# Output projection of an attention block by feature tiles over four units, with the residual as an identity in a folded matrix

## What is computed

```python
x = x + attention(cond(x, ...))          # attention ends in: out @ w_o.T + b_o
x = x + ffn(cond2(x, ...), W_base, b_base, ...)
# cond2: base = x @ W.T, plus gated low-rank terms
# ffn:   x_flat @ W_base.T + b_base, plus gated low-rank terms
```

## Time and profile before

| | us |
|---|---|
| median of 3 runs | 1196.9 |
| lowest, highest | 1192.68, 1198.27 |
| profiled execution | 1195.03 |
| its span, first to last instruction | 1193.2 |
| PE busy | 1159.9 (97%) |
| DVE, ACT, POOL busy | 720.0, 422.0, 208.4 |
| DMA | 107.79 MB, mean 90 GB/s |

### The profile page before, as it was taken

The page is one execution under the profiler, slowest core; times in us unless marked ns, Lnnn a source line. Parts: engine busy times, 40 slices in busy tenths (PEclk is TensorE's granted clock), DMA queues, the critical chain, the costliest instruction groups (busy, mean ns, idle before and its releaser), DMA issues.

```text
span 1193.2 us, 18765 instructions
## 1 busy us (share of the span) xinstructions
PE 1159.9 (97%) x6920; PEld 1040.4 (87%) x6920; DVE 720.0 (60%) x1222; ACT 422.0 (35%) x1196; POOL 208.4 (17%) x133
## 2 busy tenths in 40 slices
PE   8999999999999999999989999999999899999998
PEld 8999988888888888888879998888887688888886
DVE  5312128878788888888874227444445866666664
ACT  5212124455545555555454223212123422222221
POOL 0000114433343344444350002000000000000000
PEclk9999999999999999999999999999999899999999
DMA  6111032111111111110323114555544322222212
GB/s 251 37 37 53 9 100 80 45 45 61 44 45 51 44 44 44 44 53 26 102 80 107 55 71 169 184 173 180 178 175 159 124 107 106 106 102 85 80 71 89
DMA packets 42151, 107.79 MB, mean 90 GB/s; under 512 B 5106, under 2 KB 16242, under 8 KB 42098
## 3 DMA queue, kind: packets, MB, share of 16 engines
q1 hardware_dynamic: 42098, 107.07, 25.6%
HBM read 73.50 MB, written 33.55 MB: 90 GB/s over the span
## 4 chain that ended last, share of the span: by engine, by line
PE 91%; DVE 5%; ACT 1%; DMA 1%; issue 1%; POOL 1%; SPq 0%; DVEq 0%; ACTq 0%; POOLq 0%
PE psum L1024 22%; PE psum L1643 13%; PE psum L389 13%; PE psum L1976 13%; PE psum L1396 8%; PE psum L2037 4%; PE psum L1086 4%; PE psum L1956 4%; PE psum L1056 3%; PE psum L1071 2%; PE psum L1043 1%; PE psum L1103 1%; PE psum L1659 1%; DVE low L894 1%; DVE rows L1563 1%
## 5 line engine op out<-in xcount | busy, mean ns | idle before, releaser
L1024 PE MATMUL psum<-p_h,c_high_low 128*128 128x512 f32 (+1 forms) x768 | 196.4, 359 | 0.5 <-DVE qkv L980 0.5
L1024 PEld LDWEIGHTS psum<-p_h,c_high_low 128*128 128x128 f32 x768 | 133.5, 188 | 13.3 <-issue 0.7
L389 PE MATMUL psum<-c_high_low,w_h 128*128 128x256 f32 x768 | 135.3, 286 | 5.0 <-ACT w_h L499 4.9
L389 PEld LDWEIGHTS psum<-c_high_low,w_h 128*128 128x128 f32 x768 | 117.2, 195 | 5.2 <-issue 5.2
L1396 PE MATMUL psum<-chunk,rows 128*128 128x384 f32 (+1 forms) x576 | 107.3, 342 | 4.8 <-DVE rows L1266 2.4
L1396 PEld LDWEIGHTS psum<-chunk,rows 128*128 128x128 f32 x576 | 102.6, 190 | 5.5 <-issue 5.4
L1024 PE MATMUL psum<-p_l,c_high_low 128*128 128x512 f32 (+1 forms) x384 | 104.3, 366 | 0.0
L389 PE MATMUL psum<-c_high_low,w_l 128*128 128x256 f32 x384 | 100.3, 286 | 0.0
L1643 PE MATMUL psum<-rows,ring 128*128 128x512 f32 x384 | 93.0, 397 | 0.0
L1643 PE MATMUL psum<-rows,at 128*128 128x512 f32 x384 | 90.4, 391 | 0.0
L1643 PEld LDWEIGHTS psum<-rows,ring 128*128 128x128 f32 x384 | 71.3, 188 | 17.2 <-DVE ring L1588 0.5
(11 more groups left out here) (182 smaller groups left out, 2308.5 us busy)
## 6 DMA issues: line engine op xcount, KB each, us to landing
ring_plain<-in_x_t SPq DMA_DIRECT2D x32, 256.0 KB, 2.6
attn_scratch<-ring_plain SPq DMA_DIRECT2D x16, 512.0 KB, 2.7
scratch_plain<-attn_scratch SPq DMA_DIRECT2D x16, 512.0 KB, 5.4
x_tok<-in_x_tok SPq DMA_DIRECT2D x16, 512.0 KB, 4.3
x_scratch<-x_out SPq DMA_DIRECT2D x16, 512.0 KB, 5.9
x_t_scratch<-x_t SPq DMA_DIRECT2D x16, 512.0 KB, 2.7
raw<-x_t_scratch SPq DMA_DIRECT2D x16, 512.0 KB, 4.1
rest<-x_scratch SPq DMA_DIRECT2D x16, 512.0 KB, 4.1
```

The costliest lines, as they stand in the source:

```text
L389: mm = pe.matmul(to, stationary, moving, start=start and n == 0, stop=k == KT - 1 and n == len(passes) - 1, skip_group_check=True)
L1024: mm = pe.matmul(to, sx[:, k, :], moving(w, n, k), start=first, stop=False, skip_group_check=True)
```

## The change

The projection's operands change roles. A slice is now 128 features of the attention output for four units (128 x 512, 512 KB before as rows of 4 KB, now 256 KB in pieces of 512 bytes), and it is the moving operand; stationary is a 128x128 block of w_o. Contraction is the outermost loop inside a group of four units: for each of eight slices all eight feature tiles are multiplied, each into its own bank. The result has features on partitions, as the feed-forward wants it. Transposes, `x_scratch`, `turned`, `add_bias` and `add_base_bias` are gone. `residual` is one instruction per tile: bank + bias (one number per partition) + x, with x loaded transposed. The residual of the feed-forward is no longer added from DRAM: `FoldFFN.products` adds an identity to the folded matrix, one 128x128 matmul of `eye` with itself on the diagonal of each of eight results, and `rest` loads b_base, broadcast to all partitions. Three buffers hold split slices (SPLIT) and four the raw ones (RAW). Five weights are split ahead of the fold's last results (EARLY), three behind them. The feed-forward's first splits are spread over the last slices, the last `residual` stands behind them.

```diff
         if k == KT - 1:
+            at = self.diagonal(s, i)
+            if at is not None:
+                mm = pe.matmul(self.tile(n, width)[:, at:at + P], self.eye, self.eye, start=False, stop=True, skip_group_check=True)
             mm.then_inc(self.done, 1)
         return mm
+    def diagonal(self, s, i):
+        at = i * P - FOLD_COLS[s][1]
+        width = FOLD_COLS[s][0] - (GATED if s == 0 else 0)
+        return at + (GATED if s == 0 else 0) if 0 <= at < width and i < KT else None
...
+    ORDER = (0, 1, 5, 6, 3, 4, 2, 7)
+    BANK_OF = (0, 1, 2, 3, 7, 4, 5, 6)
+    EARLY = 5
+    GROUP = 4
+    GROUPS = UNITS // GROUP
+    SLICES = KT * GROUPS
+    SPLIT = 3
+    RAW = 4
...
-    def low_attn(self, dve, u):
-        high, low = self.at[u % 2]
-        dve.wait_ge(self.at_high, u + 1)
-        dve.tensor_tensor(low, by_tile(self.at_raw), high.bitcast(F32), ALU.subtract).then_inc(self.at_low, 1)
+            engine.wait_ge(self.at_done, (KT - 1) * (n // KT) + n % KT + 1)
+    def load_attn(self, sp, n):
+        if n >= self.RAW:
+            sp.wait_ge(self.at_low, n - self.RAW + 1)
+        source = self.a["attn"][self.units(n // KT), :, self.features(self.ORDER[n % KT])].rearrange("u p t -> p u t")
+        sp.dma_start(self.by_unit(self.raw[n % self.RAW]), source).then_inc(self.at_in[n % self.RAW], 16)
...
+        act.wait_ge(self.at_in[n % self.RAW], 16 * (n // self.RAW + 1))
+        if n >= self.SPLIT:
+            self.slice_done(act, n - self.SPLIT)
+        elif n == self.SPLIT - 1:
+            act.wait_ge(self.fold.chunk_free, self.fold.free(self.fold.STEPS - 1, 4))
+        else:
+            act.wait_ge(self.fold.chunk_low, KT * self.fold.STEPS)
+        act.activation(self.at[n % self.SPLIT][0], self.raw[n % self.RAW], ACT.Copy).then_inc(self.at_high, 1)
...
+    def load_x(self, sp, g):
+        if g > 0:
+            sp.wait_ge(self.x1_stored, 16 * KT * g)
+        for i in range(KT):
+            sp.dma_start(self.by_unit(self.x[i]), self.a["x_t"][self.units(g), :, i, :].rearrange("u p t -> p u t")).then_inc(self.x_in, 16)
...
+    def multiply(self, pe, g, m):
+        n, k = KT * g + m, self.ORDER[m]
+        pe.wait_ge(self.at_low, n + 1)
+        if g == 0:
+            pe.wait_ge(self.w_low, k + 1)
+        (ah, al), (wh, wl) = self.at[n % self.SPLIT], self.weight(k)
+        for i in range(KT):
+            if m == 0 and g == 0:
+                pe.wait_ge(self.fold.out, self.fold.TILES * self.fold.STEPS - 6 + i - (i >= HALF))
+            elif m == 0:
+                pe.wait_ge(self.x1_ready, KT * (g - 1) + i + 1)
+            cols = self.features(i)
+            for p, (w, s) in enumerate(((wh, ah), (wh, al), (wl, ah))):
+                mm = pe.matmul(self.psum[:, self.BANK_OF[i], :], w[:, cols], s, start=m == 0 and p == 0, stop=m == KT - 1 and p == 2, skip_group_check=True)
+            if m == KT - 1:
+                mm.then_inc(self.tile_done, 1)
+        if m < KT - 1:
...
+        dve.wait_ge(self.x_in, 16 * KT * (g + 1))
+        for i in range(KT):
+            dve.wait_ge(self.tile_done, KT * g + i + 1)
+            dve.scalar_tensor_tensor(self.x[i], self.psum[:, self.BANK_OF[i], :], self.bo[:, i:i + 1], self.x[i], ALU.add, ALU.add).then_inc(self.x1_ready, 1)
...
+    TURN = 9
+    BEFORE_END = wo.SLICES - wo.SPLIT - 2
...
+        sp.wait_ge(fold.chunk_low, KT * fold.STEPS)
+        for n in range(wo.RAW):
+            wo.load_attn(sp, n)
+        for k in range(KT):
+            wo.load_weight(sp, k)
+        sp.dma_start(wo.bo, wo.a["b_o"].rearrange("(k p) -> p k", p=P), allow_slow_non_contiguous=True).then_inc(wo.bo_in, 16)
+        wo.load_x(sp, 0)
+        for n in range(wo.RAW, wo.SLICES):
+            wo.load_attn(sp, n)
+            if n > KT and n % KT == wo.RAW:
+                wo.store(sp, n // KT - 1)
+            elif n > KT and n % KT == wo.RAW + 2:
+                wo.load_x(sp, n // KT)
+                if n < 2 * KT:
+                    ff.load_raw(sp, 0)
+        wo.store(sp, wo.GROUPS - 1)
...
+        for k in range(wo.EARLY, KT):
+            wo.high_weight(act, k)
+        for n in range(wo.SPLIT - 1, wo.SLICES):
+            wo.high_attn(act, n)
+            if n >= BEFORE_END:
+                ff.begin_high(act, n - BEFORE_END)
+        ff.begin_high(act, wo.SPLIT + 2)
...
+        for k in range(wo.EARLY, KT):
+            wo.low_weight(dve, k)
+        for n in range(wo.SPLIT - 1, wo.SLICES):
+            wo.low_attn(dve, n)
+            if n >= TURN and n % KT == TURN % KT:
+                wo.residual(dve, n // KT - 1)
+            if n >= BEFORE_END:
+                ff.begin_low(dve, n - BEFORE_END)
+        ff.begin_low(dve, wo.SPLIT + 2)
...
-            sp.wait_ge(self.wo.x1_biased, UNITS)
-            sp.wait_ge(self.wo.x1_turned, 2 * UNITS)
-            sp.wait_ge(self.wo.x1_stored, 16 * BPU)
+            sp.wait_ge(self.wo.x1_stored, 16 * KT * self.wo.GROUPS)
         else:
             sp.wait_ge(self.out_stored[u], 16 * p)
-        sp.dma_start(self.rest[:, u, :], self.a["x1"][BPU * p + u, :, :]).then_inc(self.rest_in[u], 16)
+        sp.dma_start(self.rest[:, u, :], self.a["b_base"].partition_broadcast(P)).then_inc(self.rest_in[u], 16)
...
+    def begin_high(self, act, n):
+        for name in (("t1",), ("t2",), ("a11", "a12"), ("a21", "a22"), ("s1", "s2"), ("s3", "s4", "t3", "t4"))[n]:
+            if name in self.TERMS:
+                self.high_term(act, self.TERMS.index(name))
+            else:
+                self.high(act, 0, name)
+    def begin_low(self, dve, n):
+        for name in ((), ("t1",), ("t2",), ("a11", "a12"), ("a21", "a22"), ())[n]:
+            if name in self.TERMS:
+                self.low_term(dve, self.TERMS.index(name))
+            else:
+                self.low(dve, 0, name)
+        for name in ((), (), (), ("s1",), ("s2",), ("s3", "s4"))[n]:
+            self.sums(dve, 0, name)
+        if n == 5:
+            for name in self.SUMS:
+                self.low(dve, 0, name)
+            self.wo.residual(dve, self.wo.GROUPS - 1)
+            self.low_term(dve, 2)
...
-        if p == 0 and name in ("p5", "p6"):
-            pe.wait_ge(self.wo.x1_t_out, 2 * UNITS)
+        if p == 0 and name == "p1":
+            pe.wait_ge(self.wo.x1_ready, self.wo.SLICES)
...
+        pe.wait_ge(wo.x1_ready, wo.SLICES - KT + BPU)
         pe.wait_ge(fold.gate2_low, 1)
         pe.wait_ge(fold.out, fold.TILES * fold.STEPS)
-        ff.gates(pe, 0, 0)
-        wo.turn(pe, UNITS - 1)
-        ff.gates(pe, 0, 1)
+        for u in range(BPU):
+            ff.gates(pe, 0, u)
```

More of the change, by code:

```diff
@@ L1171, in second_rooms @@
         z = st.enter_context(nc.sbuf_tensor("z", [P, BPU, EXP, ER], F32))
[L1172 removed]
+        eye = st.enter_context(nc.sbuf_tensor("eye", [P, P], F32R))
+    return Second(scratch, chunk, rows, gates, b11, t1, g, b22, b21, t2, t3, t4, small, z, eye)
 def middle_rooms(nc, twins):
@@ L1590, in begin_high, with store @@
+    def store(self, sp, g):
+        for i in range(KT):
+            sp.wait_ge(self.x1_ready, KT * g + i + 1)
+            sp.dma_start(self.a["x1_t"][self.units(g), :, self.features(i)].rearrange("u p t -> p u t"), self.by_unit(self.x[i])).then_inc(self.x1_stored, 16)
     def begin_high(self, act):
-        for n, k in enumerate(self.ORDER):
+        for k in range(self.EARLY):
             self.high_weight(act, k)
-            if n == 0:
-                self.high_attn(act, 0)
+            if k < self.SPLIT - 1:
+                self.high_attn(act, k)
```

278 lines of the change are left out of this document (74 added, 204 removed).

## The result

| | before | after |
|---|---|---|
| median, 4 runs each | 1197.59 us | 1177.49 us |
| lowest, highest | 1192.68, 1199.24 | 1175.81, 1177.80 |
| ratio | | 0.9836, 95% interval 0.9805 to 0.9867 |
| profiled execution, span | 1195.03, 1193.2 | 1175.81, 1174.0 |

The forecast was 1176 us, in 1170 to 1187; the sum of its steps, made against the profiled execution, was -20.6 us, and the two profiled executions differ by -19.2.

A forecast was written before the change was run, and what follows sets the result against it. PE was taken as the bound in the projection, with the seams before and behind it. Terms -13.6 + 0 + 0.9 + 2.0 - 9.9 = -20.6 us against 1196.9 gave 1176 us, range 1170 to 1187.

The forecast's parts named there:

- transposes and handovers: Projection: fifteen sets of eight transposes leave PE, 13.1 us, with about 0.5 us of handovers between units; -13.6 us.
- matmul pace: Projection: 768 matmuls before and after, start-to-start kept at 230.6 ns; 0 us, ends -2.8 and +2.2.
- identities: Folds: eight added 128-column matmuls on PE, two of them in the attention stage; +0.9 us (0.5 to 1.1).
- seam in front: Projection's start: first slice's tiles 5, 6 and 7 wait for the last three fold results; +2.0 us.
- late slices: Inside the projection: slice 15 lands at 19 us after a group's end, before PE wants it; 0 us.
- seam behind: Projection's end to the up-gates: shrinks from 29.1 to 19.2 us, -9.9 us; ends -11.3 and -2.6.
- the rest: From the first up-gate to the end: no term in the sum, so 0 us.
- 11.4 us: Projection: further shrinkage estimated from the skill's 215.7 ns at 512 columns, left out of the sum.
- near 732 to 736: Projection's start: sign expected, three short PE waits on the fold's results at these times in us.
- 288 GB/s: Projection's transfers in 512-byte pieces: full-use rate taken from the fold's loads, eight transfers in 7.3 us.
- at full clock: Seam behind the projection: sign expected, up-gates some 19 us after the last slice without the lower clock.
- Nothing on PE: Biases and scratch: rest loads the base bias instead of x1, same size and count; no PE time.

The follow-up runs named there:

- two of eight: Kernel before with two instead of eight transposes per projection unit; median 1187.19 us over 4 runs.
- raw first: Changed kernel with the next pair's raw loads at the head of the feed-forward's DMA queue; median 1174.59 us over 4 runs.
- the identity's side alone: Kernel before with only the eight identity matmuls and base bias in rest, base-bias sums and x1 stores gone; median 1195.27 us, ratio 0.9986.

## Why the prediction was right

| step | predicted | measured |
|---|---|---|
| transposes and handovers | -13.6 | -13.5 (120 x 0.111 = 13.3 from two of eight; with the pace it makes up the stage's -12.5) |
| matmul pace | 0, ends -2.8 and +2.2 | -1.0 |
| identities | +0.9 | +0.6 in the fold, by their price 0.2 ahead of it |
| seam in front | +2.0 | +2.0 |
| late slices | 0 | 0, margin 18 us |
| seam behind | -9.9 | -9.3 |
| the rest | 0 | +1.6 |

*Pace.* A slice of 24 takes 5.50 us from start to start (748.02 to 759.02 is two slices), 229.1 ns, against 230.6 predicted. By slice it is 228.8 ns with the moving values in `at`, 228.9 and 229.6 in `ring`; before, with the stationary values there, it was 227.5 and 233.4 inside a unit, 230.4 in the mean, and 768 times the 1.3 ns between them is the table's 1.0 us. So the difference by buffer is nearly gone; whether it was the buffers that made it no run here shows, for the pairs of banks alternated with them. The 215.7 ns of the Trainium skill's section Back-to-back issue gap (TensorE: Matmul & The Clock Gate), which the section gives for an isolated matmul, is reached by no slice; its 11.4 us would have been wrong by 10.

*Seam in front.* The three short waits came where they were forecast, 733.4, 734.8 and 736.2 against "near 732 to 736"; the third start is 2.0 us late, of which 1.2 are listed as waits.

*Transfers.* Slice 15 landed 19.4 us behind the group's end, 19 forecast. The form that I bounded by 288 GB/s ran at 298 at a share of 0.98. The Trainium skill's section Latency and other measured facts (DMA: Bandwidth & Descriptors) keeps 207 GB/s for a row pitch of 512 KiB from partition to partition. Here partitions are 4 KB apart, and only the four pieces of one partition are 512 KiB apart, so the prediction took the figure to a case that it was not measured for; there was no such loss.

*Seam behind.* This term was mis-sized, in two places. The up-gates came 20.0 us behind the stage, not 19.2: the last stores landed 6.4 us behind it instead of 5.2, and raw at 15.2 instead of 14.1. The up matrix, which I had left out of that queue, was issued at 909.69 while they were under way, but that it delayed them is not shown: with raw first it comes later, raw stands in its place, and they land at 6.4 all the same; without the identities it stands where it did, and they land at 5.7. And the text said "at full clock": it saw that the wait would stay but gave it no price in clock, which was +1.6 us in the rest. The pace, 1.0 us better than the forecast, made up for part of these 2.2 us; in that the closeness of the forecast is luck. The account of the seam before was off by a little, too: of the stretch of 6.8 us at the lower level (938.7 to 945.5), 1.3 lay in the wait for z, so it cost about 2.7 us and not 3.5. With that the 9.1 us from 29.1 to 20.0 come out: 5.4 less idle time (0.98 + 2.97 + 4.07 to 2.59), 0.9 of transposes, 2.7 of clock. The kernel before, by stretch (columns as in the earlier trace rows):

```profile
938.80:940.00 1.20, 0.00 (x0) 0.00 (x0) 1.03 (x6) 0.92 (x2) 0.00 (x0) 0.50 0.00 0
940.00:945.40 5.40, 5.39 (x14) 4.33 (x15) 4.90 (x8) 1.10 (x3) 0.00 (x0) 0.50 0.00 0
945.60:948.30 2.70, 2.70 (x13) 2.23 (x12) 0.69 (x1) 1.12 (x2) 0.00 (x0) 1.00 0.00 0
```

*What the parts are worth.* The stage's 12.5 us come with the form of the projection. Of the seam's 9.3, the identity's side alone gave 3.3 in one trace of the kernel before, at 0.8 on PE, and 2.5 of them hang on where the lower clock fell; in ten runs it was worth 0.1 to 3.1 us in all. The form of the projection without the identity was not run, so the seam's gain is not divided further. The prediction's "Nothing on PE" for biases and scratch left out the 0.8 us by which z comes earlier without the bias sum.

## What to carry to other kernels

Price each wait that a change leaves, not only those that it removes: here 2.6 us of waiting cost 4.2, and a DMA issued three places earlier gave 3.5 of it back. Where the granted clock reacts to waits, a microsecond removed on another engine can be worth three or none, so read gains by stage, from stage to stage of the traces, and look at the granted clock of each stage before trusting a median. And try a suspected limit of transfers by adding traffic until it bites: that gives the margin in microseconds.

## What I had not expected of the hardware

The lower clock does not follow every equal wait. Behind the wait of 2.97 us ahead of the last transposes the kernel before stayed at the full level, and three variants of it, with 2.96 to 2.98, did not. Ahead of the up-gates, waits of 2.4 to 2.7 us were followed by it five times in five; three waits of 1.8 to 1.9 (two there, one ahead of z) were not. The stretch at the lower level cost 1.6 to 3.1 us there and 2.7 in the projection. In the attention stage a wait of 2.65 us stands in every trace at the same place of the program, and the lower level followed it in ten of fourteen, in one of the two traces of the same changed kernel and not in the other. That alone makes executions of one program differ by about a microsecond.
